# Half-size transfers in turn, five chunks ahead, and one chunk at a time on VectorE

## The chip, the core and the metric

The kernel runs on one core of one Trainium2 chip. The metric is the device time of one execution in microseconds (us), lower is better. A core has five engines that run their own instruction queues and meet at semaphores: TensorE (PE in the profile), VectorE (DVE), ScalarE (ACT), GpSimd (POOL) and SyncE (SP), which here only issues DMA transfers.

## What is computed

`x` has shape (2048, 64, 16, 16) in fp32: 2048 images of 64 channels and 16 x 16 pixels, 134 MB. Each image is normalised in groups of two neighbouring channels, goes through a hexagonal convolution (three 4 x 4 kernels with five taps each and a stride of 2, after a border that is filled by wrapping pixels around), is masked, and is added to the input:

```python
def _gn(v, G=32, eps=1e-5):           # groups of 2 channels x 256 pixels
    g = v.reshape(B_, G, C_ // G, H_, W_)
    m, s = mean(g), var(g)            # over (2, 3, 4)
    return ((g - m) / jnp.sqrt(s + eps)).reshape(v.shape)

xp = pad(x, 1); xp = xp.at[:, :, DST_R, DST_C].set(xp[:, :, SRC_R, SRC_C])
up    = conv(xp, w_up    * UP,    b_up)       # 4x4, stride 2, 5 taps used
left  = conv(xp, w_left  * LEFT,  b_left)
right = conv(xp, w_right * RIGHT, b_right)
out[:, :, 0::2, 0::2], out[:, :, 1::2, 0::2], out[:, :, 1::2, 1::2] = up, left, right
return x + out * OUT_MASK             # with x = _gn(x) as conv input
```

The input is read once and the output, of the same size, written once: 269 MB in all.

## The kernel before, in words

The images are cut into 64 chunks (`NCHUNK`) of 32 images. A chunk lies in SBUF as 128 partitions (two images x 64 channels) by 16 pairs (`G`) of 256 pixels, 2 MB. `xs` has 8 slots (`SLOTS`) for chunks; a chunk is loaded into its slot, its results are added to it in place, and the slot is stored. The stages of a chunk k are these.

- SP issues every transfer. `load` (L182) fetches one chunk in one transfer; `store` (L186) waits until GpSimd has added all four banks of the chunk (`bank_added`) and writes it. After store k, the load of chunk k + 7 waits for the store of chunk k - 1 (L211, the same slot). The first chunk comes in quarters. The bias vectors come in six tiny transfers on the same queue, behind chunk 2 (L202).
- VectorE takes the statistics: eight `bn_stats` (L233) for a chunk. `moments` (L237) makes the variance from them in six small operations on 128 x 16 (or 48) values, ScalarE takes the square root (`root`, L312), and `norms` (L258) makes the factor and the offset in five more. Each of them that needs the one before waits on a semaphore. The `bn_stats` of chunk k + 1 are written between these small operations of chunk k (`bn(ahead, ...)`), so `stats` has two buffers.
- `normalise` writes the normalised chunk into one of two buffers `tn`: pairs 0 to 7 on VectorE (L281), 8 to 15 on ScalarE (L320). It waits until the convolution of chunk k - 2 has read that buffer (`wait_t_free`, L158).
- GpSimd wraps the border with five copies (`wrap`, L414).
- TensorE (L462) runs 240 matmuls for a chunk into four PSUM banks; there are two sets of four, one for even, one for odd chunks. Banks 0 and 1 are full halfway, banks 2 and 3 at the end. A tiny matmul (L473) opens each chunk.
- ScalarE empties a bank with the bias into `res` (`evacuate`, L343, ten activations for a chunk). `res` holds one chunk, so it waits until GpSimd has added the same bank of the chunk before.
- GpSimd adds `res` to the slot in `xs` (`add`, L404, twelve strided tensor_tensor operations).

The order of the work is written out by hand. ScalarE: root k, evacuate k - 2, normalise k. GpSimd: add k - 2, wrap k. VectorE: moments k, norms k (both with the statistics of k + 1 in between), normalise k. The small operations of VectorE that this document counts are L241 (shuffle), L245, L246, L247, L249, L254 (variance), then after the root L262 (reciprocal), L265, L269, L272, L276 (offset).

Of the kernel before, what the change touches and what calls it, by code (L numbers as in the profile page):

```python
# [7 lines left out]
F32 = mybir.dt.float32  # L8
# [5 lines left out]
P = 128  # L14
B, C, HW = 2048, 64, 16
PIX = HW * HW
G = 16
NCHUNK = B // (2 * G)
SLOTS = 8
LAG = 2  # L20
# [41 lines left out]


QUARTER = G // 4


WRAPS = [
# [22 lines left out]
def hex_conv(nc, x, w_up, b_up, w_left, b_left, w_right, b_right, out):  # L90
    ctx = ExitStack()
    with ctx:
        def sb(name, shape, dt):
            return ctx.enter_context(nc.sbuf_tensor(name, shape, dt))

        def sem(name):
            return ctx.enter_context(nc.semaphore(name))
# [8 lines left out]
        ident = sb("ident", [P, C], F32)  # L106
        blank = sb("blank", [P, P], F16)
        bias = sb("bias", [P, 3], F32)
        stats = sb("stats", [P, 2, G, 3], F32)
        mate = sb("mate", [P, G, 3], F32)  # L110
        gap = sb("gap", [P, G], F32)
        gap2 = sb("gap2", [P, G], F32)
# [16 lines left out]
            at = 2 * C * 16 + C * (NT * W_AT[t][1] + n)  # L129
            return tn[1][W_AT[t][0]:W_AT[t][0] + C, at:at + C]  # L130

        loaded = [sem(f"loaded{s}") for s in range(SLOTS)]
        stored = [sem(f"stored{s}") for s in range(SLOTS)]
        w_loaded = [sem(f"w_loaded{t}") for t in range(3)]
        b_loaded = sem("b_loaded")
        quarter = [sem(f"quarter{n}") for n in range(3)]
        cleared = sem("cleared")
        identity = sem("identity")
        edges_clear = sem("edges_clear")
# [39 lines left out]

        @block.sync  # L180
        def _(sp):
            def load(k):  # L182
                s = k % SLOTS
                sp.dma_start(xs[:, s, :].rearrange("p (g q) -> p g q", g=G), x_dram[k]).then_inc(loaded[s], 16)

            def store(k):  # L186

                s = k % SLOTS
                sp.wait_ge(bank_added, NB * (k + 1))
                sp.dma_start(out_dram[k], xs[:, s, :].rearrange("p (g q) -> p g q", g=G)).then_inc(stored[s], 16)  # L190

            for t, w in enumerate((w_up, w_left, w_right)):
                sp.dma_start(w_raw(t), w.rearrange("o c a b -> o (c a b)")).then_inc(w_loaded[t], 16)
            for n in range(4):
                pairs = slice(QUARTER * n, QUARTER * (n + 1))
                sp.dma_start(xs[:, 0, :].rearrange("p (g q) -> p g q", g=G)[:, pairs],
                             x_dram[0][:, pairs]).then_inc(quarter[n] if n < 3 else loaded[0], 16)
            load(1)
            load(2)
            for t, b in enumerate((b_up, b_left, b_right)):  # L200
                for h in range(2):
                    sp.dma_start(bias[C * h:C * h + C, t:t + 1],  # L202
                                 b.rearrange("(o a) -> o a", a=1)).then_inc(b_loaded, 16)

            for k in range(3, SLOTS):
                load(k)

            for k in range(NCHUNK - 1):
                store(k)
                if 0 < k < NCHUNK - SLOTS + 1:  # L210
                    sp.wait_ge(stored[(k - 1) % SLOTS], 16 * ((k - 1) // SLOTS + 1))  # L211
                    load(k + SLOTS - 1)
            for half in range(2):
                pairs = slice(G // 2 * half, G // 2 * (half + 1))
                sp.wait_ge(bank_added, NB * NCHUNK + 2 * half)
                sp.dma_start(out_dram[NCHUNK - 1][:, pairs],
                             xs[:, SLOTS - 1, :].rearrange("p (g q) -> p g q", g=G)[:, pairs]
                             ).then_inc(stored[SLOTS - 1], 16)
            for s in range(SLOTS):
                sp.wait_ge(stored[s], 16 * (NCHUNK // SLOTS + (s == SLOTS - 1)))  # L220

        @block.vector
        def _(dve):
            def bn(k, u0, u1):

                if k >= NCHUNK:
                    return
                s = k % SLOTS
                if u0 == 0 and k:
                    dve.wait_ge(loaded[s], 16 * (k // SLOTS + 1))  # L230
                for u in range(u0, u1):
                    both = view(xs, (s * G + 2 * u) * PIX, [(1, PIX), (PIX, 2)])
                    last = nc.vector.bn_stats(stats[:, k % 2, 2 * u:2 * u + 2].rearrange("p g a -> p (g a)"), both)  # L233
                if u1 == G // 2:
                    last.then_inc(bn_done, 1)

            def moments(k, ahead):  # L237

                done = STAT_OPS * k
                own = stats[:, k % 2]  # L240
                nc.vector.stream_shuffle(mate[:].rearrange("p g a -> p (g a)"), own.rearrange("p g a -> p (g a)"),  # L241
                                         [p ^ 1 for p in range(32)]).then_inc(stat_step, 1)
                bn(ahead, 0, 1)
                dve.wait_ge(stat_step, done + 1)
                nc.vector.tensor_tensor(gap[:], own[:, :, 1], mate[:, :, 1], ALU.subtract).then_inc(stat_step, 1)  # L245
                nc.vector.tensor_tensor(m2[:], own[:, :, 2], mate[:, :, 2], ALU.add).then_inc(stat_step, 1)  # L246
                nc.vector.tensor_tensor(msum[:], own[:, :, 1], mate[:, :, 1], ALU.add).then_inc(stat_step, 1)  # L247
                dve.wait_ge(stat_step, done + 2)
                nc.vector.scalar_tensor_tensor(gap2[:], gap[:], float(PIX // 2), gap[:],  # L249
                                               op0=ALU.mult, op1=ALU.mult).then_inc(stat_step, 1)  # L250
                bn(ahead, 1, 2)
                dve.wait_ge(stat_step, done + 5)

                nc.vector.scalar_tensor_tensor(var[:], gap2[:], EPS * GROUP, m2[:],  # L254
                                               op0=ALU.add, op1=ALU.add).then_inc(var_ready, 1)
                bn(ahead, 2, 4)

            def norms(k, ahead):  # L258

                done = STAT_OPS * k + 5  # L260
                dve.wait_ge(std_ready, k + 1)
                nc.vector.reciprocal(small[:, 0], std[:]).then_inc(stat_step, 1)  # L262
                bn(ahead, 4, 5)
                dve.wait_ge(stat_step, done + 1)
                nc.vector.scalar_tensor_tensor(small[:, 1], var[:], -0.5 / GROUP, small[:, 0],  # L265
                                               op0=ALU.mult, op1=ALU.mult).then_inc(stat_step, 1)
                bn(ahead, 5, 6)
                dve.wait_ge(stat_step, done + 2)
                nc.vector.tensor_tensor(small[:, 2], small[:, 1], small[:, 0], ALU.mult).then_inc(stat_step, 1)  # L269
                bn(ahead, 6, 7)  # L270
                dve.wait_ge(stat_step, done + 3)
                nc.vector.scalar_tensor_tensor(rstd[:], small[:, 2], 1.5, small[:, 0],  # L272
                                               op0=ALU.add, op1=ALU.mult).then_inc(stat_step, 1)
                bn(ahead, 7, 8)
                dve.wait_ge(stat_step, done + 4)
                nc.vector.scalar_tensor_tensor(nmr[:], msum[:], -0.5, rstd[:],  # L276
                                               op0=ALU.mult, op1=ALU.mult).then_inc(norm_ready, 1)
# [10 lines left out]
                t_pairs(k % 2, k % SLOTS, 0, pairs).then_inc(t_dve, 1)  # L288

            for n in range(4):  # L290
                if n < 3:
                    dve.wait_ge(quarter[n], 16)
                else:
                    dve.wait_ge(loaded[0], 16)
                bn(0, QUARTER // 2 * n, QUARTER // 2 * (n + 1))
            dve.wait_ge(bn_done, 1)
            moments(0, NCHUNK)
            norms(0, NCHUNK)
            normalise(0, GD0)
            bn(1, 0, G // 2)  # L300
            dve.wait_ge(bn_done, 2)

            for k in range(1, NCHUNK):
                moments(k, k + 1)
                norms(k, k + 1)
                normalise(k)
                if k + 1 < NCHUNK:
                    dve.wait_ge(bn_done, k + 2)

        @block.scalar  # L310
        def _(act):
            def root(k):  # L312
                act.wait_ge(var_ready, k + 1)
                nc.scalar.activation(std[:], var[:], ACT.Sqrt, scale=1.0 / GROUP).then_inc(std_ready, 1)  # L314
# [15 lines left out]
            def evacuate(k, b, j):  # L330
# [15 lines left out]
                    at += cols  # L346
                last.then_inc(bank_empty, 1)

            act.wait_ge(identity, 1)
            nc.scalar.activation(warm[:], ident[0:C, 0:1], ACT.Sqrt)  # L350
            for t in range(3):
# [5 lines left out]
            root(0)  # L357
            normalise(0, GD0)

            root(1)  # L360
            normalise(1, GD)
            act.wait_ge(b_loaded, 16 * 6)
            for k in range(LAG, NCHUNK):
                root(k)
                for j in range(NB):
                    evacuate(k - LAG, k % 2, j)
                normalise(k, GD)
            for k in range(NCHUNK - LAG, NCHUNK):
                for j in range(NB):
                    evacuate(k, k % 2, j)  # L370

        @block.gpsimd
        def _(pool):
# [141 lines left out]
```

## Time and profile before

| | |
|---|---|
| median of 3 runs | 743.91 us (743.77 to 744.04) |
| profiled execution: time, span | 743.65 us, 741.8 us (granted TensorE clock 0.993) |
| busy PE / DVE / ACT / POOL | 656.3 / 667.6 / 574.5 / 487.5 us |
| DMA | 269.6 MB, mean 363 GB/s over the span |
| DMA busy share by 40ths | 9 tenths or more in all but the last slice (6) |

The profile is of one execution. Its time lies 1.85 us above its span (743.65 less 741.8) and 0.26 us below the median of the runs. Busy times are a union of an engine's instructions; an instruction that waits for something inside the engine still counts as busy, so a longer duration of the same operation at another place is a wait too. A timeline row gives start, duration, engine, line, operation, output and input, and in brackets how long the engine was idle before it and what ended that.

### The profile page before, as it was taken

To read this page: it belongs to the slowest core of one execution; us is meant where nothing else is said; L and a number is where in the kernel's file an instruction comes from. 1 tells how busy PE (TensorE), PEld (TensorE's weight loads), DVE (VectorE), ACT (ScalarE), POOL (GpSimd) and SP (SyncE) were. 2 spreads that over 40 slices of the span, in tenths; PEclk is the share of its full clock that TensorE was granted. 3 is DMA by queue.
4 is the path that set the end of the run, shared out by engine and by line. 5 is a ranking of instruction groups with operands and counts; after the bars stand their busy time and mean duration, and the time that the engine had idled before them with its cause. 6 is when DMAs were issued, how large, how long until landed. Compare 5 with 4: busy or idle time off the path is not lost.

```text
span 741.8 us, 35919 instructions
## 1 busy us (share of the span) xinstructions
PE 656.3 (88%) x15484; PEld 602.5 (81%) x15484; DVE 667.6 (90%) x1793; ACT 574.5 (77%) x1235; POOL 487.5 (66%) x1109
## 2 busy tenths in 40 slices
PE   1699999999998898898898988988988988989893
PEld 1589999999887887887887887878878878878883
DVE  4999999999889999999999999999999999999940
ACT  3398888888787787787787877877877877878782
POOL 1178777778567576676675675676766766766784
PEclk9999999999999999999999999999999999999998
DMA  9999999999999999999999999999999999999996
GB/s 275 339 349 380 379 376 372 373 360 364 362 374 378 369 372 373 369 377 371 374 363 376 380 368 374 369 374 369 375 377 364 378 365 378 370 373 374 369 327 229
DMA packets 265017, 269.60 MB, mean 363 GB/s; under 512 B 2640, under 2 KB 264784, under 8 KB 264976
## 3 DMA queue, kind: packets, MB, share of 16 engines
q1 hardware_dynamic: 264976, 269.23, 105.8%
q14 instruction: 37, 0.30, 0.1%
q8 instruction: 4, 0.07, 0.0%
HBM read 135.01 MB, written 134.22 MB: 363 GB/s over the span
## 4 chain that ended last, share of the span: by engine, by line
DMA 70%; DVE 18%; POOL 3%; PE 3%; ACT 2%; SPq 1%; issue 1%; POOLq 0%; ACTq 0%
DMA xs<-in_x 43%; DMA out<-xs 27%; DVE stats L233 9%; DVE tn L281 4%; POOL xs L404 3%; PE bank L462 3%; ACT res L343 1%; ACT tn L320 1%; DVE small L265 1%; DVE rstd L272 1%; SPq L190 1%; DVE nmr L276 0%; DVE small L269 0%; DVE m L246 0%; POOL tn L414 0%
## 5 line engine op out<-in xcount | busy, mean ns | idle before, releaser
L462 PE MATMUL bank<-tn,wts 64*64 64x192 f32 (+1 forms) x15360 | 647.0, 325 | 0.0
L462 PEld LDWEIGHTS bank<-tn,wts 64*64 64x64 f32 x15360 | 593.1, 137 | 34.5
L404 POOL TENSOR_TENSOR xs<-res,xs 128x192 f32<-128x192 f32 (+6 forms) x775 | 387.4, 539 | 71.5 <-ACT res L343 70.9
L233 DVE BATCH_NORM_STATS2 stats<-xs 128x6 f32<-128x512 f32 x512 | 347.2, 691 | 43.2 <-DMA xs<-in_x 43.2
L343 ACT ACTIVATE res<-bank,bias 64x512 f32<-64x512 f32 (+5 forms) x640 | 302.0, 472 | 17.3 <-PE bank L462 7.6
L320 ACT ACTIVATE tn<-xs,nmr,rstd 128x256 f32<-128x256 f32 x511 | 258.9, 591 | 9.2 <-DVE nmr L276 7.7
L414 POOL COPY tn<-tn 128x128 f32<-128x128 f32 (+2 forms) x320 | 97.6, 361 | 168.7 <-ACT tn L320 168.7
L281 DVE TENSOR_SCALAR tn<-xs,rstd,nmr 128x256 f32<-128x256 f32 x513 | 197.2, 454 | 2.3
L314 ACT ACTIVATE std<-var 128x16 f32<-128x16 f32 x64 | 13.8, 216 | 127.4 <-DVE var L254 127.4
L473 PEld LDWEIGHTS bank<-blank 128*128 128x128 f16 x64 | 6.1, 95 | 86.4 <-issue 82.6
L473 PE MATMUL bank<-blank 128*128 128x2 f16 x64 | 11.2, 175 | 67.6 <-POOL tn L414 67.6
L265 DVE SCALAR_TENSOR_TENSOR small<-var,small 128x16 f32<-128x16 f32 x64 | 30.4, 475 | 0.1
L272 DVE SCALAR_TENSOR_TENSOR rstd<-small 128x16 f32<-128x16 f32 x64 | 28.1, 438 | 0.1
L276 DVE SCALAR_TENSOR_TENSOR nmr<-msum,rstd 128x16 f32<-128x16 f32 x64 | 22.7, 355 | 0.1
L246 DVE TENSOR_TENSOR m<-stats,mate 128x16 f32<-128x16 f32 x64 | 21.8, 340 | 0.0
L247 DVE TENSOR_TENSOR msum<-stats,mate 128x16 f32<-128x16 f32 x64 | 21.1, 330 | 0.0
L249 DVE SCALAR_TENSOR_TENSOR gap<-gap 128x16 f32<-128x16 f32 x64 | 16.2, 254 | 0.0
L262 DVE RECIPROCAL small<-std 128x16 f32<-128x16 f32 x64 | 14.9, 233 | 0.7 <-ACT std L314 0.7
L245 DVE TENSOR_TENSOR gap<-stats,mate 128x16 f32<-128x16 f32 x64 | 14.1, 221 | 0.1
L269 DVE TENSOR_TENSOR small<-small 128x16 f32<-128x16 f32 x64 | 14.0, 219 | 0.1
L241 DVE STREAM_SHUFFLE mate<-stats 128x48 f32<-128x48 f32 x64 | 12.8, 201 | 0.0
L254 DVE SCALAR_TENSOR_TENSOR var<-gap,m 128x16 f32<-128x16 f32 x64 | 11.2, 175 | 0.1
(18 smaller groups left out, 17.0 us busy)
## 6 DMA issues: line engine op xcount, KB each, us to landing
xs<-in_x SPq DMA_DIRECT2D x63, 2048.0 KB, 16.8
out<-xs SPq DMA_DIRECT2D x63, 2048.0 KB, 17.0
xs<-in_x SPq DMA_DIRECT2D x4, 512.0 KB, 7.8
out<-xs SPq DMA_DIRECT2D x2, 1024.0 KB, 5.2
tn<-in_L_conv_w_up SPq DMA_DIRECT2D x1, 256.0 KB, 3.6
tn<-in_L_conv_w_left SPq DMA_DIRECT2D x1, 256.0 KB, 4.0
tn<-in_L_conv_w_right SPq DMA_DIRECT2D x1, 256.0 KB, 5.2
bias<-in_L_conv_b_up SPq DMA_DIRECT2D x2, 0.2 KB, 8.6
```

Source lines behind the costliest of these rows:

```text
L233: last = nc.vector.bn_stats(stats[:, k % 2, 2 * u:2 * u + 2].rearrange("p g a -> p (g a)"), both)
L246: nc.vector.tensor_tensor(m2[:], own[:, :, 2], mate[:, :, 2], ALU.add).then_inc(stat_step, 1)
L247: nc.vector.tensor_tensor(msum[:], own[:, :, 1], mate[:, :, 1], ALU.add).then_inc(stat_step, 1)
L265: nc.vector.scalar_tensor_tensor(small[:, 1], var[:], -0.5 / GROUP, small[:, 0], op0=ALU.mult, op1=ALU.mult).then_inc(stat_step, 1)
L272: nc.vector.scalar_tensor_tensor(rstd[:], small[:, 2], 1.5, small[:, 0], op0=ALU.add, op1=ALU.mult).then_inc(stat_step, 1)
L276: nc.vector.scalar_tensor_tensor(nmr[:], msum[:], -0.5, rstd[:], op0=ALU.mult, op1=ALU.mult).then_inc(norm_ready, 1)
L281: last = nc.vector.tensor_scalar(t_image(b, g), x_image(s, g), rstd[:, g:g + 1], nmr[:, g:g + 1], ALU.mult, ALU.add)
L320: last = nc.scalar.activation(t_image(k % 2, g), x_image(k % SLOTS, g), ACT.Identity, bias=nmr[:, g:g + 1], scale=rstd[:, g:g + 1])
L343: last = nc.scalar.activation(res[onto, BANK_AT[j] + at:BANK_AT[j] + at + cols], psum[NB * b + j][banks, at:at + cols], ACT.Identity, bias ...
L404: last = nc.gpsimd.tensor_tensor(onto, frm, onto, ALU.add)
L414: last = nc.gpsimd.tensor_copy(view(tn[b], dst, [(T_PAIR, G)] + [(d, n) for d, _, n in dims]), view(tn[b], src, [(T_PAIR, G)] + [(d, n) fo ...
L462: last = nc.tensor.matmul(psum[bank + j][to:to + C, at:at + cols], wts[first:first + C, NT * rect[0] + n, :], taps(b, rect, tap, first), s ...
```

## The change

SP now moves every chunk in two halves of eight pairs (1 MB each) with a semaphore for each half of a slot. Chunks 0 to 4 are asked for at the start (`AHEAD` = 5). After that SP issues for each chunk k: store of the first half of k, load of the first half of k + 5, store of the second half, load of the second half. Both halves of a store wait for the whole chunk, except for the last chunk. A load of chunk n waits for the store of chunk n - 8, which is k - 3. The bias vectors move to ScalarE's DMA queue, ahead of its first instruction.

VectorE no longer takes the statistics of the next chunk between the small operations. For each chunk it waits for a half, takes four `bn_stats`, waits for the other, takes four, then does moments, norms and normalise, and only then goes to the next chunk.

ScalarE's order becomes root k, normalise k, evacuate k - 1. GpSimd's and TensorE's code is unchanged.

```diff
+HALF = (slice(0, G // 2), slice(G // 2, G))
+AHEAD = 5
 ...
-        stats = sb("stats", [P, 2, G, 3], F32)
+        stats = sb("stats", [P, G, 3], F32)
 ...
+            for k in range(1, AHEAD):
+                for half in range(2):
+                    load(k, half)
+
+            for k in range(NCHUNK):
+                n = k + AHEAD
+                for half in range(2):
+                    sp.wait_ge(bank_added, NB * (k + 1) if k < NCHUNK - 1 else NB * k + 4 + 2 * half)
+                    store(k, half)
+                    if n < NCHUNK:
+                        if n >= SLOTS:
+                            sp.wait_ge(stored[n % SLOTS], 32 * (n // SLOTS))
+                        load(n, half)
 ...
-            def moments(k, ahead):
+            def moments(k):
                 done = STAT_OPS * k
-                own = stats[:, k % 2]
+                own = stats
+                dve.wait_ge(bn_done, k + 1)
                 nc.vector.stream_shuffle(mate...)
-                bn(ahead, 0, 1)
 ...
             for k in range(1, NCHUNK):
-                moments(k, k + 1)
-                norms(k, k + 1)
+                for half in range(2):
+                    dve.wait_ge(loaded[half][k % SLOTS], 16 * (k // SLOTS + 1))
+                    bn(k, G // 4 * half, G // 4 * (half + 1))
+                moments(k)
+                norms(k)
                 normalise(k)
 ...
-            root(1)
-            normalise(1, GD)
             act.wait_ge(b_loaded, 16 * 6)
-            for k in range(LAG, NCHUNK):
+            for k in range(1, NCHUNK):
                 root(k)
+                normalise(k, GD)
                 for j in range(NB):
-                    evacuate(k - LAG, k % 2, j)
-                normalise(k, GD)
-            for k in range(NCHUNK - LAG, NCHUNK):
-                for j in range(NB):
-                    evacuate(k, k % 2, j)
+                    evacuate(k - 1, (k - 1) % 2, j)
+            for j in range(NB):
+                evacuate(NCHUNK - 1, (NCHUNK - 1) % 2, j)
```

## Rows read from the trace of the kernel before

**Rows 1.** Windows: length, busy time by engine, granted clock, DMA share, GB/s.
```profile
15.00:20.00 5.00, 0.00 (x0) 0.00 (x0) 4.47 (x20) 2.98 (x7) 0.00 (x0) 1.00 1.10 349
...
200.00:690.00 490.00, 439.93 (x10412) 403.58 (x10412) 459.42 (x1217) 384.89 (x822) 328.35 (x738) 1.00 1.07 372
```

**Rows 2.** Waits from 200 to 700 us: total, times, longest.
```profile
DVE stats L233 <- DMA xs<-in_x: 31.1, 45, 1.3
```

**Rows 3.** Timeline of the first chunk, with nothing else between: start, duration, instruction.
```profile
14.94 0.20 DVE L241 STREAM_SHUFFLE mate<-stats 128x48 f32<-128x48 f32 x1
15.18 0.18 DVE L245 TENSOR_TENSOR gap<-stats,mate 128x16 f32<-128x16 f32 x1
...
15.65 0.17 DVE L254 SCALAR_TENSOR_TENSOR var<-gap,m 128x16 f32<-128x16 f32 x1
15.86 0.22 ACT L314 ACTIVATE std<-var 128x16 f32<-128x16 f32 x1 [5.68 <-DVE var L254]
16.11 0.25 DVE L262 RECIPROCAL small<-std 128x16 f32<-128x16 f32 x1 [0.28 <-ACT std L314]
16.40 0.18 DVE L265 SCALAR_TENSOR_TENSOR small<-var,small 128x16 f32<-128x16 f32 x1
...
17.24 3.00 DVE L281 TENSOR_SCALAR tn<-xs,rstd,nmr 128x256 f32<-128x256 f32 x9
20.15 4.92 DVE L233 BATCH_NORM_STATS2 stats<-xs 128x6 f32<-128x512 f32 x8
...
22.69 12.22 PE L462 MATMUL bank<-tn,wts 64*64 64x288 f32 x240
...
25.11 0.20 DVE L241 STREAM_SHUFFLE mate<-stats 128x48 f32<-128x48 f32 x1
25.80 0.70 DVE L233 BATCH_NORM_STATS2 stats<-xs 128x6 f32<-128x512 f32 x1 [0.48 <-DMA xs<-in_x]
```

**Rows 4.** Timeline of a period in the middle: normalise, wrap, VectorE beside it.
```profile
342.50 3.08 DVE L281 TENSOR_SCALAR tn<-xs,rstd,nmr 128x256 f32<-128x256 f32 x8
...
346.75 1.49 POOL L414 COPY tn<-tn 128x128 f32<-128x128 f32 x5 [2.29 <-ACT tn L320]
...
347.12 0.42 DVE L246 TENSOR_TENSOR m<-stats,mate 128x16 f32<-128x16 f32 x1
347.46 0.42 DVE L247 TENSOR_TENSOR msum<-stats,mate 128x16 f32<-128x16 f32 x1
```

**Rows 5.** Timeline of GpSimd alone, the third copy of that wrap.
```profile
347.45 0.41 POOL L414 COPY tn<-tn 128x128 f32<-128x128 f32 x1
```

**Rows 6.** Timeline of the same period: convolution, emptying, a small operation.
```profile
348.49 10.05 PE L462 MATMUL bank<-tn,wts 64*64 64x288 f32 x240
...
348.94 4.87 ACT L343 ACTIVATE res<-bank,bias 128x480 f32<-128x480 f32 x10
...
350.65 0.47 DVE L265 SCALAR_TENSOR_TENSOR small<-var,small 128x16 f32<-128x16 f32 x1
```

**Rows 7.** Timeline of GpSimd: adds 1 to 3, 4 to 8, 10 to 12 of that chunk.
```profile
349.66 2.04 POOL L404 TENSOR_TENSOR xs<-res,xs 128x288 f32<-128x288 f32 x3 [1.41 <-ACT res L343]
...
351.64 2.51 POOL L404 TENSOR_TENSOR xs<-res,xs 128x192 f32<-128x192 f32 x5
...
354.55 1.19 POOL L404 TENSOR_TENSOR xs<-res,xs 128x64 f32<-128x64 f32 x3
```

**Rows 8.** Timeline at the last chunk, whose small operations stand alone on VectorE.
```profile
707.96 1.51 POOL L414 COPY tn<-tn 128x128 f32<-128x128 f32 x5 [2.33 <-ACT tn L320]
...
708.26 0.18 DVE L265 SCALAR_TENSOR_TENSOR small<-var,small 128x16 f32<-128x16 f32 x1
708.47 0.27 DVE L269 TENSOR_TENSOR small<-small 128x16 f32<-128x16 f32 x1
...
709.35 4.98 DVE L281 TENSOR_SCALAR tn<-xs,rstd,nmr 128x256 f32<-128x256 f32 x8
```

**Rows 9.** Timeline of GpSimd in the same stretch, the first eight adds.
```profile
709.42 4.76 POOL L404 TENSOR_TENSOR xs<-res,xs 128x288 f32<-128x288 f32 x8
```

**Rows 10.** Timeline: two bias transfers on SP, and the last convolution.
```profile
20.28 1.24 SPq L202 DMA_DIRECT2D bias<-in_L_conv_b_left  x2
...
719.79 10.07 PE L462 MATMUL bank<-tn,wts 64*64 64x288 f32 x240
```

More of the change, by code:

```diff
@@ L130, in w_used @@
             return tn[1][W_AT[t][0]:W_AT[t][0] + C, at:at + C]
-        loaded = [sem(f"loaded{s}") for s in range(SLOTS)]
+        loaded = [[sem(f"loaded{s}_{half}") for s in range(SLOTS)] for half in range(2)]
         stored = [sem(f"stored{s}") for s in range(SLOTS)]
@@ L135, in hex_conv @@
         b_loaded = sem("b_loaded")
-        quarter = [sem(f"quarter{n}") for n in range(3)]
+        quarter = [sem(f"quarter{n}") for n in range(2)]
         cleared = sem("cleared")
@@ L181, in _, with part, load, store @@
         def _(sp):
[L182 to L190, printed above, removed]
+            def part(dram, k, pairs):
+                return dram[k][:, pairs], xs[:, k % SLOTS, :].rearrange("p (g q) -> p g q", g=G)[:, pairs]
+            def load(k, half):
+                frm, to = part(x_dram, k, HALF[half])
+                sp.dma_start(to, frm).then_inc(loaded[half][k % SLOTS], 16)
+            def store(k, half):
+                to, frm = part(out_dram, k, HALF[half])
+                sp.dma_start(to, frm).then_inc(stored[k % SLOTS], 16)
             for t, w in enumerate((w_up, w_left, w_right)):
@@ L194, in _ @@
             for n in range(4):
[L195 to L218, printed above, removed]
+                frm, to = part(x_dram, 0, slice(QUARTER * n, QUARTER * (n + 1)))
+                sp.dma_start(to, frm).then_inc((quarter[n // 2], loaded[n // 2][0])[n % 2], 16)
+            for k in range(1, AHEAD):
[10 more added lines that the diff above has]
+                        load(n, half)
             for s in range(SLOTS):
-                sp.wait_ge(stored[s], 16 * (NCHUNK // SLOTS + (s == SLOTS - 1)))
+                sp.wait_ge(stored[s], 32 * (NCHUNK // SLOTS))
         @block.vector
@@ L224, in bn @@
             def bn(k, u0, u1):
-                if k >= NCHUNK:
-                    return
                 s = k % SLOTS
-                if u0 == 0 and k:
-                    dve.wait_ge(loaded[s], 16 * (k // SLOTS + 1))
                 for u in range(u0, u1):
                     both = view(xs, (s * G + 2 * u) * PIX, [(1, PIX), (PIX, 2)])
-                    last = nc.vector.bn_stats(stats[:, k % 2, 2 * u:2 * u + 2].rearrange("p g a -> p (g a)"), both)
+                    last = nc.vector.bn_stats(stats[:, 2 * u:2 * u + 2].rearrange("p g a -> p (g a)"), both)
                 if u1 == G // 2:
                     last.then_inc(bn_done, 1)
-            def moments(k, ahead):
+            def moments(k):
                 done = STAT_OPS * k
-                own = stats[:, k % 2]
-                nc.vector.stream_shuffle(mate[:].rearrange("p g a -> p (g a)"), own.rearrange("p g a -> p (g a)"),
+                own = stats
+                dve.wait_ge(bn_done, k + 1)
+                nc.vector.stream_shuffle(mate[:].rearrange("p g a -> p (g a)"), own[:].rearrange("p g a -> p (g a)"),
                                          [p ^ 1 for p in range(32)]).then_inc(stat_step, 1)
-                bn(ahead, 0, 1)
                 dve.wait_ge(stat_step, done + 1)
@@ L250, in moments @@
                                                op0=ALU.mult, op1=ALU.mult).then_inc(stat_step, 1)
-                bn(ahead, 1, 2)
                 dve.wait_ge(stat_step, done + 5)
@@ L255, in moments, with norms @@
                                                op0=ALU.add, op1=ALU.add).then_inc(var_ready, 1)
-                bn(ahead, 2, 4)
-            def norms(k, ahead):
+            def norms(k):
                 done = STAT_OPS * k + 5
@@ L262, in norms @@
                 nc.vector.reciprocal(small[:, 0], std[:]).then_inc(stat_step, 1)
-                bn(ahead, 4, 5)
                 dve.wait_ge(stat_step, done + 1)
@@ L266, in norms @@
                                                op0=ALU.mult, op1=ALU.mult).then_inc(stat_step, 1)
-                bn(ahead, 5, 6)
                 dve.wait_ge(stat_step, done + 2)
                 nc.vector.tensor_tensor(small[:, 2], small[:, 1], small[:, 0], ALU.mult).then_inc(stat_step, 1)
-                bn(ahead, 6, 7)
                 dve.wait_ge(stat_step, done + 3)
@@ L273, in norms @@
                                                op0=ALU.add, op1=ALU.mult).then_inc(stat_step, 1)
-                bn(ahead, 7, 8)
                 dve.wait_ge(stat_step, done + 4)
@@ L290, in _ @@
             for n in range(4):
[L291 to L294, printed above, removed]
+                dve.wait_ge((quarter[n // 2], loaded[n // 2][0])[n % 2], 16)
                 bn(0, QUARTER // 2 * n, QUARTER // 2 * (n + 1))
-            dve.wait_ge(bn_done, 1)
-            moments(0, NCHUNK)
-            norms(0, NCHUNK)
+            moments(0)
+            norms(0)
             normalise(0, GD0)
-            bn(1, 0, G // 2)
-            dve.wait_ge(bn_done, 2)
             for k in range(1, NCHUNK):
-                moments(k, k + 1)
-                norms(k, k + 1)
+                for half in range(2):
[3 more added lines that the diff above has]
+                norms(k)
                 normalise(k)
-                if k + 1 < NCHUNK:
-                    dve.wait_ge(bn_done, k + 2)
         @block.scalar
@@ L347, in evacuate @@
                 last.then_inc(bank_empty, 1)
+            for t, b in enumerate((b_up, b_left, b_right)):
+                for h in range(2):
+                    act.dma_start(bias[C * h:C * h + C, t:t + 1],
+                                 b.rearrange("(o a) -> o a", a=1)).then_inc(b_loaded, 16)
             act.wait_ge(identity, 1)
```

## The prediction

> **What bounds the kernel now.** I read the time windows first. From 200 to 690 us the DMA engines are busy throughout and move 372 GB/s; when only loads ran, at 15 to 20 us, it was 349 [rows 1]. A chunk is 2.097 MB in and as much out, so 4.194 MB / 372 GB/s = 11.27 us is what a chunk costs in transfers. The view of waits says the same from the other side: VectorE's first `bn_stats` of a chunk waits for its load once per chunk, 31.1 us in 45 chunks, 0.69 us each [rows 2]. VectorE could therefore go round in 11.27 - 0.69, about 10.6 us at most. TensorE needs 10.05 us for a chunk [rows 6]. So DMA is the bound, and three engines stand less than 1.3 us behind it. Any change to VectorE's loop must be asked whether it still fits into 11.27 us.
>
> **VectorE's new loop, without company.** I count from N, the start of a chunk's normalise on VectorE, to the same point a chunk later. The first chunk of the kernel before shows each piece with nothing between. Nine tensor_scalars from 17.24 to 20.15 are 0.323 us each, so eight take 2.59. Eight `bn_stats` from 20.15 to the shuffle at 25.11: 4.96. Shuffle to L245, 14.94 to 15.18: 0.24. L245 to normalise, 15.18 to 17.24: 2.06, the trip to ScalarE's root included [all rows 3]. Sum 9.85 us. On this count the loop fits, and DMA stays the bound. It is the count I don't believe, for the following reason.
>
> **VectorE beside GpSimd.** L246 and L247 take 0.42 us each in the middle of the run, start 0.34 us apart, and run beside wrap copies of 0.41 us, the third of which starts at 347.45 when L247 starts at 347.46 [rows 4, 5]. In the first chunk, with GpSimd idle, four of them and a wait fit between 15.18 and 15.65, about 0.12 us each [rows 3]. So VectorE's small operations with two inputs take turns with GpSimd's: one for one. Beside adds it is the same: L265 takes 0.47 instead of 0.18 [rows 6, 3], and the last chunk's eight tensor_scalars take 4.98 us beside eight adds of 4.76, against 2.59 alone [rows 8, 9, 3]. `bn_stats` is not touched: the eight from 20.15 on keep their pace though a wrap ran in the middle of them. What the interleaving bought was this: the small operations were spread, one between two `bn_stats` of 0.62 us, so that GpSimd's turn passed behind a `bn_stats`. The change puts nine two-input operations in a row.
>
> The Trainium skill (SBUF — State Buffer, "Who interferes with whom") says that a VectorE instruction with two SBUF inputs, or in a two-port mode, and a GpSimd instruction that reads SBUF shut each other out for the whole instruction, and that one with a single input outside those modes doesn't. The trace agrees, by the 0.42 against 0.17 to 0.18 us above.
>
> **Where GpSimd will be.** Its code is the same, but add k - 1 no longer waits for ScalarE to pass the next root: the banks are emptied straight after normalise. N to the start of wrap is 342.50 to 346.75, 4.25 us; the wrap takes 1.49 [rows 4]; the adds then follow at N + 5.75, since by then ScalarE has emptied bank 0 (about 0.7 us after its normalise ends). The first three adds take until 351.64, 1.98 us; adds 4 to 8 2.5; the last three end 6.08 us after the first began [rows 7]. So adds run from N + 5.75 to N + 11.83. VectorE reaches L245 at N + 2.59 + 4.96 + 0.24 = N + 7.79, just after add 4 began (N + 7.73). Then, turn by turn:
> - L245, L246, L247, L249, L254 end with adds 4 to 8, at N + 10.2 (351.64 + 2.51 is 4.49 after the first add; less the 0.05 by which neighbours overlap). Alone they took 0.64.
> - The root and back: from L254's end at 15.82 to L262's start at 16.11, 0.29, and L262 to L265 0.29 more [rows 3]: N + 10.8.
> - L265, L269, L272 end with adds 10, 11, 12: the last at N + 11.83. L276 is free again: 0.2, and normalise starts at **N + 12.05**.
>
> The neighbours: ScalarE's ten activations take 4.87 [rows 6], from N + 4.1 to N + 9.0, ahead of the root at N + 10.2: covered by 1.2 us. TensorE starts a chunk 1.74 us after the wrap began (346.75 to 348.49 [rows 4, 6]) and ends 10.05 later, N + 16.0; bank 2 is wanted at N + 12.05 + 4.1 + 2.1 = N + 18.3, so it may be 2.2 us slower and cost nothing. The waits for a free `tn` buffer and for `res` are long past by then. Period 12.05 against 11.27: VectorE with GpSimd becomes the bound.
>
> The value hangs on which add VectorE meets first. One turn earlier gives 11.85, one turn later about 12.25; these are the bounds.
>
> **The transfers.** At 12.05 us a chunk DMA idles 0.8 us of it. A load is issued when chunk k is added, N(k+1) + 11.8, and lands with its store at most 11.3 later; it is wanted at N(k+4) + 2.6, that is N(k+1) + 38.7. Five ahead are enough. What halves do to the rate no row shows. The lower bound I take is all at the one-directional 349 GB/s: 12.02 us a chunk, still under 12.05. A gain in rate would be worth nothing. At the start, chunk 2 has landed by 25.80 [rows 3]; two more at 349 GB/s, 6.0 us each, end at 37.8, then DMA idles until the first store near 39.5. That costs nothing either, as chunk 5 is wanted only past 66. The six bias issues take 0.62 us each on a queue [rows 10], 3.7 us on ScalarE at the start; ScalarE stood idle 5.68 us ahead of the first root [rows 3], which covers it. Without that cover it would be up to 3.7 once.
>
> **The sum.** N(0) = 17.24. N(1) = 20.15 + 4.96 + 0.24 + 2.06 = 27.41, no adds yet. The first convolution ends at 34.91 [rows 3] and holds ScalarE back a little, I add 0.2. Then 62 periods: 27.41 + 0.2 + 62 x 12.05 = 774.7. From the last normalise to the end: 4.25 + 1.74 + 10.07, and from the end of the convolution (719.79 + 10.07 = 729.86 [rows 10]) to the end of the span, 741.84, 11.98: 28.04. Span 802.7; with the 1.85 between span and time 804.6. Against the profiled execution's 743.65 that is +61; its time lies 0.26 under the median of the runs, which doesn't matter here. Forecast **804 us**, with periods of 11.85 to 12.25: 792 to 817.
>
> **The rivals.**
> - *GpSimd gives way (faster).* If it is the adds that wait for the VectorE operations and not the reverse, the loop takes 9.85 us, DMA bounds again, and the change gains at the end: the first store at 39.5, then 59 loads and 59 stores of 5.635 us end at 704; four `bn_stats` (2.5) and 2.3 more put N(63) at 709; +28.0 +1.85 = 739 us. This decides as soon as VectorE's loop stays below 11.27 us, so if turns cost it under 1.4 us instead of 2.2. For it speaks L265 at 708.26, which slipped in ahead of a copy and took 0.18 [rows 8]; against it L269 behind it with 0.27, and the 4.98 us of the tensor_scalars. The same page of the Trainium skill says that the one that issues first holds the pair. 6%.
> - *Half of the turns slip.* As at 708.26, dependent operations get in ahead at times. With three or four turns spared the period is about 11.4: 27.6 + 62 x 11.4 + 28.0 + 1.85 = 764 us. 12%.
> - *DMA loses with halves, or the turns cost more.* Alternating 1 MB transfers drop the rate below 348 GB/s, or adds stretched by VectorE's operations lengthen the row of turns (eight took 4.76 here against 4.49 in the middle, [rows 9, 7]): period 12.5, 832 us. 9%.
> - *TensorE slows.* It idles 2 us of each period; at half its clock for part of it, a convolution could pass 12.2 us. From 12.3 on it sets the period; 13 us would give 863. 3%.
> - *The change does nothing that counts*: DMA-bound with the old ends, 742 to 744: 2%.
>
> The forecast itself has 68%. Low and high reach to periods of 11.55 and 12.4: 775 and 827; this leaves out about 20%. About 0.2% is what runs of this kernel can tell from no change. Faster 0.06, same 0.02, slower 0.92.
>
> **What the changed profile would show.** The share of DMA falls to 0.93 or so of its earlier value and GB/s to about 348. VectorE's wait for loads goes to nearly nothing, and the chain of work runs through VectorE's small operations and GpSimd's adds. L245 to L254 have durations of 0.35 to 0.65 us, L276 about 0.2. The distance between two normalise groups on VectorE is 12.05. ScalarE's root waits for the variance, never for its own emptying. If `bn_stats` still waits for loads every chunk, the forecast is wrong.

## The result and the profile after

The changed kernel takes 794.3 us (793.38 to 795.26, 4 runs) against 743.97 for the kernel before in the same runs: ratio 1.067, 95% interval 1.066 to 1.069. The profiled execution took 793.74 us with a span of 791.9. The forecast was 804, slower, with a range of 775 to 827.

The page of the changed kernel: span, GB/s in 40 slices, and the shares of the chain of work that ended last.

```profile
span 791.9 us, 36045 instructions
...
GB/s 264 309 316 361 349 351 361 348 354 357 351 346 366 354 347 362 357 348 359 357 348 356 351 351 359 356 350 353 351 348 363 353 355 354 357 345 359 269 212 212
...
DVE 91%; issue 2%; ACT 2%; PE 1%; DMA 1%; POOL 1%; SPq 0%; POOLq 0%; ACTq 0%
```

Of the kernel before, the chain was this:

```profile
DMA 70%; DVE 18%; POOL 3%; PE 3%; ACT 2%; SPq 1%; issue 1%; POOLq 0%; ACTq 0%
```

It ran over DMA for 70% of the span; now VectorE has 91% of it. The transfers fell from 372 GB/s in the middle [rows 1] to 354, because less was asked of them (4.194 MB in each loop of 11.86 us):

```profile
200.00:690.00 490.00, 437.84 (x9922) 397.56 (x9926) 466.36 (x1158) 367.50 (x787) 299.62 (x706) 0.95 1.06 354
```

The view of waits has no line any more for VectorE's `bn_stats` waiting for a load in the middle of the run (31.1 us before [rows 2]). One round of the loop, VectorE, ScalarE and GpSimd's adds (the lines are numbered anew: L235 to L243 are the old L245 to L254, L250 to L260 the old L262 to L276, L265 the old L281, L223 the `bn_stats`, L384 the adds):

```profile
401.70 5.76 POOL L384 TENSOR_TENSOR xs<-res,xs 128x288 f32<-128x288 f32 x12
...
403.89 0.40 DVE L235 TENSOR_TENSOR gap<-stats,mate 128x16 f32<-128x16 f32 x1
404.21 0.54 DVE L236 TENSOR_TENSOR m<-stats,mate 128x16 f32<-128x16 f32 x1
404.67 0.66 DVE L237 TENSOR_TENSOR msum<-stats,mate 128x16 f32<-128x16 f32 x1
405.25 0.43 DVE L239 SCALAR_TENSOR_TENSOR gap<-gap 128x16 f32<-128x16 f32 x1
405.71 0.40 DVE L243 SCALAR_TENSOR_TENSOR var<-gap,m 128x16 f32<-128x16 f32 x1
406.14 0.22 ACT L293 ACTIVATE std<-var 128x16 f32<-128x16 f32 x1 [1.29 <-DVE var L243]
406.39 0.25 DVE L250 RECIPROCAL small<-std 128x16 f32<-128x16 f32 x1 [0.28 <-ACT std L293]
406.68 0.50 DVE L252 SCALAR_TENSOR_TENSOR small<-var,small 128x16 f32<-128x16 f32 x1
407.21 0.28 DVE L255 TENSOR_TENSOR small<-small 128x16 f32<-128x16 f32 x1
...
407.52 0.17 DVE L257 SCALAR_TENSOR_TENSOR rstd<-small 128x16 f32<-128x16 f32 x1
407.73 0.18 DVE L260 SCALAR_TENSOR_TENSOR nmr<-msum,rstd 128x16 f32<-128x16 f32 x1
...
407.95 2.68 DVE L265 TENSOR_SCALAR tn<-xs,rstd,nmr 128x256 f32<-128x256 f32 x8
```

The adds run from 401.70 to 407.46. Every two-input operation that falls in that time is long (0.40 to 0.66, and 0.50 and 0.28), and the two behind its end take 0.17 and 0.18, as in the first chunk of the kernel before [rows 3]. GpSimd's adds one by one, numbers 4, 8, 11 and 12 of the twelve:

```profile
403.63 0.62 POOL L384 TENSOR_TENSOR xs<-res,xs 128x192 f32<-128x192 f32 x1
...
405.61 0.47 POOL L384 TENSOR_TENSOR xs<-res,xs 128x128 f32<-128x128 f32 x1
...
406.74 0.41 POOL L384 TENSOR_TENSOR xs<-res,xs 128x96 f32<-128x96 f32 x1
407.11 0.35 POOL L384 TENSOR_TENSOR xs<-res,xs 128x64 f32<-128x64 f32 x1
```

Each of VectorE's long operations ends 0.03 to 0.04 us after one of them: L235 at 404.29 after add 4 (404.25), L243 at 406.11 after add 8 (406.08), L252 at 407.18 after add 11 (407.15), L255 at 407.49 after add 12 (407.46); L236, L237 and L239 go with adds 5, 6 and 7 in the same way. ScalarE waited 1.29 us for the variance, so it wasn't late. N(k) is the start of VectorE's normalise of chunk k, as in the prediction. N(1) is 28.30 and N(63) is 763.90 in this trace, so the loop is (763.90 - 28.30) / 62 = 11.86 us.

### The profile page after: what moved, and what is told of

Same layout as the page of the kernel before. It is cut to its first block, busy times and chain, and to the rows that moved or that the text cites. A ratio compares the mean times of both kernels' runs of the same rounds, so it can differ in the third digit from the quotient of the medians.

```text
span 791.9 us, 36045 instructions
## 1 busy us (share of the span) xinstructions
PE 684.1 (86%) x15484; PEld 621.4 (78%) x15484; DVE 719.4 (91%) x1793; ACT 574.1 (72%) x1235; POOL 466.1 (59%) x1109
## 4 chain that ended last, share of the span: by engine, by line
DVE 91%; issue 2%; ACT 2%; PE 1%; DMA 1%; POOL 1%; SPq 0%; POOLq 0%; ACTq 0%
DVE stats L223 39%; DVE tn L265 21%; DVE msum L237 4%; DVE small L252 4%; DVE m L236 4%; DVE var L243 3%; DVE gap L235 3%; DVE gap L239 3%; DVE small L255 2%; DVE small L250 2%; ACT std L293 2%; DVE mate L232 2%; DVE rstd L257 2%; DVE nmr L260 2%; PE bank L442 1%
## 5 line engine op out<-in xcount | busy, mean ns | idle before, releaser
L442 PE MATMUL bank<-tn,wts 64*64 64x192 f32 (+1 forms) x15360 | 674.0, 333 | 0.0
L442 PEld LDWEIGHTS bank<-tn,wts 64*64 64x64 f32 x15360 | 612.0, 141 | 42.6
L384 POOL TENSOR_TENSOR xs<-res,xs 128x192 f32<-128x192 f32 (+6 forms) x775 | 369.2, 521 | 3.6 <-ACT res L322 3.5
L223 DVE BATCH_NORM_STATS2 stats<-xs 128x6 f32<-128x512 f32 x512 | 318.0, 697 | 10.5 <-DMA xs<-in_x 10.5
L265 DVE TENSOR_SCALAR tn<-xs,rstd,nmr 128x256 f32<-128x256 f32 x513 | 171.8, 410 | 2.6 <-DVE nmr L260 0.3
L237 DVE TENSOR_TENSOR msum<-stats,mate 128x16 f32<-128x16 f32 x64 | 40.6, 634 | 0.0
L236 DVE TENSOR_TENSOR m<-stats,mate 128x16 f32<-128x16 f32 x64 | 33.9, 530 | 0.0
L250 DVE RECIPROCAL small<-std 128x16 f32<-128x16 f32 x64 | 16.2, 253 | 18.1 <-ACT std L293 18.1
L252 DVE SCALAR_TENSOR_TENSOR small<-var,small 128x16 f32<-128x16 f32 x64 | 28.7, 448 | 2.2
L243 DVE SCALAR_TENSOR_TENSOR var<-gap,m 128x16 f32<-128x16 f32 x64 | 25.2, 394 | 2.2
L239 DVE SCALAR_TENSOR_TENSOR gap<-gap 128x16 f32<-128x16 f32 x64 | 26.8, 419 | 0.0
L235 DVE TENSOR_TENSOR gap<-stats,mate 128x16 f32<-128x16 f32 x64 | 24.7, 386 | 2.2
L255 DVE TENSOR_TENSOR small<-small 128x16 f32<-128x16 f32 x64 | 17.5, 273 | 2.2
L257 DVE SCALAR_TENSOR_TENSOR rstd<-small 128x16 f32<-128x16 f32 x64 | 11.9, 186 | 2.2
L260 DVE SCALAR_TENSOR_TENSOR nmr<-msum,rstd 128x16 f32<-128x16 f32 x64 | 11.3, 177 | 2.2
## 6 DMA issues: line engine op xcount, KB each, us to landing
xs<-in_x SPq DMA_DIRECT2D x126, 1024.0 KB, 10.8
```

The costliest lines, as they stand in the source:

```text
L223: last = nc.vector.bn_stats(stats[:, 2 * u:2 * u + 2].rearrange("p g a -> p (g a)"), both)
L265: last = nc.vector.tensor_scalar(t_image(b, g), x_image(s, g), rstd[:, g:g + 1], nmr[:, g:g + 1], ALU.mult, ALU.add)
L384: last = nc.gpsimd.tensor_tensor(onto, frm, onto, ALU.add)
L442: last = nc.tensor.matmul(psum[bank + j][to:to + C, at:at + cols], wts[first:first + C, NT * rect[0] + n, :], taps(b, rect, tap, first), s ...
```

## The experiments

All times are medians; the ratio is to the kernel before in the same runs.

| run | time, us | ratio (95%) |
|---|---|---|
| the change | 794.3 | 1.067 (1.066 to 1.069) |
| no_adds (doesn't compute the result) | 740.6 | 0.996 (0.994 to 0.997) |
| interleave | 816.9 | 1.102 (1.096 to 1.109) |
| gd7 | 800.5 | 1.076 (1.074 to 1.078) |
| gd9 | 781.0 | 1.050 (1.048 to 1.051) |
| gd10 | 785.5 | 1.056 (1.055 to 1.058) |
| no_newton (leaves out a step of accuracy) | 748.7 | 1.006 (1.004 to 1.007) |
| scalar_undone | 824.4 | 1.107 (1.106 to 1.109) |
| vector_alone | 823.2 | 1.106 (1.104 to 1.108) |
| transfers_alone | 761.5 | 1.024 (1.022 to 1.025) |
| transfers_7 | 741.3 | 0.996 (0.995 to 0.998) |
| change_7 | 795.2 | 1.069 (1.067 to 1.070) |
| short_row | 743.3 | 1.000 (0.998 to 1.001) |

The theory to be tested ("turns"): each two-input operation of VectorE that meets GpSimd's adds waits for one of them to end, and a row of nine such operations makes VectorE's loop longer than DMA's 11.27 us. The rivals: the row is slow by itself; VectorE is simply full; the transfers; ScalarE's new order. The edits shift the line numbers of some runs by a few; the names of the tiles tell which operation a row shows.

**Without the adds.**

```diff
             def add(k, j, g0=0, pairs=G):
+                nc.gpsimd.memset(sink[:, at0:at0 + 1], 0.0).then_inc(bank_added, 1)
+                return
```

> The changed kernel without GpSimd's additions: each bank's twelve-part add is replaced by a write of one value to a scratch column that signals the same semaphore, so the output is the input alone (the convolution is computed and not added). Turn theory: the nine two-input operations take 0.17 to 0.18 us each, the loop would be 9.9 us, so DMA bounds at 11.27: 735 to 742 us. Rival (the row of dependent operations and the trip to ScalarE's root is what costs, GpSimd is not in it): the period stays 11.9 and the time 790 to 795.

Measured: 740.6 us. VectorE in the middle of that run:

```profile
403.44 2.53 DVE L224 BATCH_NORM_STATS2 stats<-xs 128x6 f32<-128x512 f32 x4 [1.26 <-DMA xs<-in_x]
...
406.26 0.18 DVE L236 TENSOR_TENSOR gap<-stats,mate 128x16 f32<-128x16 f32 x1
...
408.31 2.67 DVE L266 TENSOR_SCALAR tn<-xs,rstd,nmr 128x256 f32<-128x256 f32 x8
```

From the first small operation to normalise it takes 2.05 us (406.26 to 408.31), where the changed kernel takes 4.06 (403.89 to 407.95). So 2.0 us of each loop belong to GpSimd's adds, and without them VectorE waits for loads again (1.26 us). The row by itself is not slow.

**VectorE gets less or more to do.** `GD` is the number of pairs that VectorE normalises; ScalarE has the rest of the sixteen.

```diff
-GD = 8
+GD = 7      # gd7;  9 in gd9, 10 in gd10
```

> The changed kernel with VectorE normalising seven pairs of a chunk and ScalarE nine. Turn theory: VectorE comes to its small operations 0.3 us earlier and the adds start 0.5 us later, so it meets the third to the seventh and then the ninth to the twelfth: period 12.0, 802 us, though VectorE has less work. Rival (VectorE is simply full): 0.32 x 62 = 20 us less, 774 us.

> The changed kernel with VectorE normalising ten pairs of a chunk and ScalarE six, instead of eight and eight. Turn theory: ScalarE ends about 1 us earlier, so wrap and adds start about 1 us earlier against VectorE, which itself comes to its small operations 0.65 us later; it meets the last six adds only (from the seventh on), and its last four small operations are free: period 11.5, 768 us. Rival (VectorE is simply full, work added to it is time added): 0.65 x 62 = 40 us more, 834 us.

> The changed kernel with nine pairs on VectorE and seven on ScalarE. Turn theory: wrap at N + 3.7, adds at N + 5.2, the first small operation at N + 8.2 in the sixth add, five turns to the tenth, then one in the twelfth, three free: loop 11.65 us, 780 us. Rival (VectorE is simply full): 794 + 20 = 814 us.

Measured: 800.5, 785.5 and 781.0 us. "VectorE is simply full" gave 774, 834 and 814; it has the wrong sign three times. With one pair less the kernel is 6 us slower, with one pair more 13 us faster. The forecasts of the turns (802 for seven pairs, 768 for ten, 780 for nine) hold for seven and nine. In gd7 the adds start later and still run when the last small operation comes, which isn't free any more:

```profile
405.13 5.72 POOL L384 TENSOR_TENSOR xs<-res,xs 128x288 f32<-128x288 f32 x12
...
410.60 0.28 DVE L260 SCALAR_TENSOR_TENSOR nmr<-msum,rstd 128x16 f32<-128x16 f32 x1
```

In gd9 the period is 413.35 - 401.69 = 11.66 us:

```profile
401.69 3.00 DVE L265 TENSOR_SCALAR tn<-xs,rstd,nmr 128x256 f32<-128x256 f32 x9
...
405.38 1.50 POOL L394 COPY tn<-tn 128x128 f32<-128x128 f32 x5 [4.45 <-ACT tn L299]
406.84 5.75 POOL L384 TENSOR_TENSOR xs<-res,xs 128x288 f32<-128x288 f32 x12
...
409.84 0.62 DVE L235 TENSOR_TENSOR gap<-stats,mate 128x16 f32<-128x16 f32 x1
...
412.51 0.18 DVE L252 SCALAR_TENSOR_TENSOR small<-var,small 128x16 f32<-128x16 f32 x1
...
413.35 1.06 DVE L265 TENSOR_SCALAR tn<-xs,rstd,nmr 128x256 f32<-128x256 f32 x3
```

The wrap and the adds come earlier, since ScalarE has seven pairs, and after the root all four small operations are free (0.18). For ten pairs the forecast was 17 us too low. The trace shows a thing that it had wrong: the wrap waits for both halves of the normalised chunk, and now VectorE's half ends last.

```profile
404.38 3.32 DVE L265 TENSOR_SCALAR tn<-xs,rstd,nmr 128x256 f32<-128x256 f32 x10
...
407.77 1.50 POOL L394 COPY tn<-tn 128x128 f32<-128x128 f32 x5 [4.52 <-DVE tn L265]
```

I had counted ScalarE's six pairs alone, 3.07 us; the wrap starts at N + 3.39 instead. These 0.3 us in 62 chunks have the size of the miss, but no run tells them from the rest of that forecast, whose period of 11.5 was not worked out turn by turn.

**Three of the nine taken out.**

```diff
-                nc.vector.reciprocal(small[:, 0], std[:]).then_inc(stat_step, 1)
-                ... small[:, 1], small[:, 2] and rstd from it
+                nc.vector.reciprocal(rstd[:], std[:]).then_inc(stat_step, 1)
```

> The changed kernel without the refinement of 1/sqrt: three two-input operations of norms are taken out and the reciprocal goes straight to rstd. It computes the same but a step of accuracy. Turn theory: VectorE's loop becomes 11.87 - 0.8 = 11.1 us, just under DMA's 11.27, so DMA bounds and the time is 738 to 744 us. Rival (ScalarE's ring or GpSimd sets the 11.9): 790 us or more.

Measured: 748.7 us. The first and the last normalise of the loop on VectorE:

```profile
27.18 2.67 DVE L257 TENSOR_SCALAR tn<-xs,rstd,nmr 128x256 f32<-128x256 f32 x8
...
720.47 2.67 DVE L257 TENSOR_SCALAR tn<-xs,rstd,nmr 128x256 f32<-128x256 f32 x8
```

(720.47 - 27.18) / 62 = 11.18 us, 0.1 above what was worked out and 0.68 less than in the changed kernel. The rival's 790 is out. The total is above the 738 to 744, because I let DMA set it. VectorE's loop still sets the end, with its start of 27.2 and its tail of 28.0, and has 88% of the chain in the page of this run, DMA 1%.

The kernel before doesn't go round in 11.27 us from the start: its normalise of chunk 1 begins at 31.64 and that of chunk 16 at 183.60, 10.13 us a chunk, on loads that lie ready. A loop of 11.18 us can't catch up in that way.

**ScalarE's order undone, and VectorE's part alone.**

The edit of scalar_undone:

```diff
-            for k in range(1, NCHUNK):
+            for k in range(LAG, NCHUNK):
                 root(k)
+                for j in range(NB):
+                    evacuate(k - LAG, k % 2, j)
                 normalise(k, GD)
 ...
-                    evacuate(k - 1, (k - 1) % 2, j)
```

vector_alone is the kernel before with `moments(k)` and `norms(k)` of the change, so with no `bn_stats` between the small operations.

> The changed kernel with ScalarE's order alone undone: root k, evacuate k - 2, normalise k. Turn theory, from the root: adds begin 0.85 us after it, so two small operations and all eight tensor_scalars take turns with adds (normalise ends 6.35 after the root instead of 3.6), then bn_stats 4.96, and the variance is free: period 12.2, 817 us with the later wrap at the end. Rival (ScalarE's new order is what slows the change): below 794, down to 745.

> The kernel before with VectorE's part of the change alone: one chunk at a time, whole transfers, ScalarE's old order. Turn theory: as with ScalarE's order undone, 12.2 us a chunk, 815 to 820 us; the transfers make no difference. Rival (transfers matter): more than 5 us from that run.

Measured: 824.4 us, 7 above the forecast, and 823.2, 3 above the upper end of its range, and within 2 us of each other though one has half transfers five ahead and the other whole ones. ScalarE's new order is therefore worth 30 us to the change (824.4 to 794.3), by where it puts the adds:

```profile
400.53 4.95 DVE L223 BATCH_NORM_STATS2 stats<-xs 128x6 f32<-128x512 f32 x8
...
405.76 0.18 DVE L235 TENSOR_TENSOR gap<-stats,mate 128x16 f32<-128x16 f32 x1
...
407.30 6.25 POOL L387 TENSOR_TENSOR xs<-res,xs 128x288 f32<-128x288 f32 x12 [2.45 <-ACT res L322]
407.41 0.76 DVE L257 SCALAR_TENSOR_TENSOR rstd<-small 128x16 f32<-128x16 f32 x1
408.20 0.53 DVE L260 SCALAR_TENSOR_TENSOR nmr<-msum,rstd 128x16 f32<-128x16 f32 x1
408.77 4.17 DVE L265 TENSOR_SCALAR tn<-xs,rstd,nmr 128x256 f32<-128x256 f32 x8
...
412.87 0.70 DVE L223 BATCH_NORM_STATS2 stats<-xs 128x6 f32<-128x512 f32 x1
```

Here the variance is free (0.18), but two small operations and the eight tensor_scalars (4.17 us instead of 2.68) take turns: 412.87 - 400.53 = 12.34 us a chunk.

**VectorE's part undone.**

```diff
-            def moments(k):
+            def moments(k, ahead):
 ...
+                bn(ahead, 0, 1)
                 dve.wait_ge(stat_step, done + 1)
```

> The changed kernel with VectorE's part alone undone: the statistics of the next chunk stand between the small operations again, with two stats buffers. Halves, five ahead, ScalarE's order and the bias queue stay. Turn theory: the turns pass behind bn_stats, the loop of VectorE falls to about 10.3 us and DMA bounds at 11.27 us a chunk; some 738 us, 0.993 of the kernel before. Rival (halves or five ahead starve the transfers): 760 to 795, VectorE waiting for loads and DMA idle in the middle.

Measured: 816.9 us where 738 was expected, the largest miss of all runs: worse than the change, and neither by turns nor, for the most part, by the transfers; in its middle VectorE waits for no load. What goes round is ScalarE's work and the root's way through VectorE:

```profile
409.97 4.05 ACT L312 ACTIVATE tn<-xs,nmr,rstd 128x256 f32<-128x256 f32 x8 [3.08 <-DVE nmr L270]
...
413.93 4.86 ACT L335 ACTIVATE res<-bank,bias 128x480 f32<-128x480 f32 x10
...
418.81 0.22 ACT L306 ACTIVATE std<-var 128x16 f32<-128x16 f32 x1
...
422.14 4.05 ACT L312 ACTIVATE tn<-xs,nmr,rstd 128x256 f32<-128x256 f32 x8 [3.11 <-DVE nmr L270]
```

In the new order ScalarE empties banks ahead of the root, and normalise hangs on the root by way of VectorE's five operations. Normalise 3.96, emptying 4.88, then root to normalise 3.33: 12.17 us, a ring with no slack in it. The 3.33 are long because four `bn_stats` stand among the five operations; in the changed kernel the same way takes 1.81 (406.14 to 407.95). The small operations themselves are short again, though the adds run from 403.46 to 409.20:

```profile
403.46 5.74 POOL L397 TENSOR_TENSOR xs<-res,xs 128x288 f32<-128x288 f32 x12
...
408.39 0.16 DVE L263 TENSOR_TENSOR small<-small 128x16 f32<-128x16 f32 x1
```

So the turns did pass behind `bn_stats`, as expected, and the time was lost elsewhere. Emptying ahead of the root, with the statistics between, is the worse pairing; the two parts of the change belong together. That ring is what the next run tells from the transfers.

**The transfers alone** (the run above, with ScalarE's old order as well).

> The kernel before with the transfers of the change alone: halves in turn, five ahead, bias on ScalarE's queue; VectorE's statistics between the small operations and ScalarE's order (root, evacuate k - 2, normalise) as before. Ring theory: without ScalarE's new order nothing but DMA is near 11.27 us; the time is DMA's, 738 to 743 us. Rival (it was the transfers that made the run with the statistics interleaved slow, not ScalarE's order): 800 us or more.

Measured: 761.5 us. ScalarE's order accounts for 55 us of the run above (816.9 to 761.5), as the ring theory says, but this is 17 us above the kernel before, which it doesn't say. Of this run a window at the start, a wait in the middle, and the GB/s of the page:

```profile
36.00:46.00 10.00, 8.99 (x171) 8.15 (x175) 9.96 (x29) 8.80 (x20) 7.28 (x18) 0.83 0.35 114
```
```profile
DVE stats L227 <- DMA xs<-in_x: 85.6, 43, 2.3
```
```profile
GB/s 264 331 234 383 384 384 376 369 367 371 367 360 368 374 365 367 371 370 366 372 371 366 368 370 371 371 369 368 368 368 365 376 367 366 370 369 369 348 226 221
```

DMA is at 0.35 of its time for 10 us: the five chunks are in, and the first store is issued at 42.76. So I tried the depth by itself:

```diff
-AHEAD = 5
+AHEAD = 7
```

> The run with the transfers alone, but seven chunks ahead instead of five. Depth theory: with ScalarE emptying chunk k - 2 a chunk lives longer, and five ahead leaves DMA idle before the first store and loads late by 2 us in each chunk; with seven the time is that of the kernel before, 740 to 746 us. Rival (it is the halves that cost): it stays near 761.

> The changed kernel with seven chunks ahead instead of five. Turn theory: VectorE waits for no load in the middle, so the depth is worth nothing: 794 us, within 2. Rival (the depth or late loads hold the change back): below 788.

Measured: 741.3 with the transfers alone, 795.2 in the change. The five ahead cost 20 us in the one and nothing that can be measured in the other, since the change stores earlier and its VectorE waits for no load. With seven ahead the halves are even a little faster than the kernel before, 0.996 (0.995 to 0.998), though in the middle they move no more: 368 GB/s against 372 [rows 1]. The gain is at the ends. The page of this run:

```profile
GB/s 265 348 362 384 385 372 378 379 366 377 370 353 372 364 372 371 365 373 366 371 372 368 369 368 363 376 366 369 375 366 368 364 364 376 366 368 372 377 355 284
```

The last two slices are 355 and 284 GB/s; they were 327 and 229 in the kernel before. VectorE still waits for loads, 84.9 us in all between 200 and 700 us, as much as with five ahead (85.6), so that wait is not what the depth costs. The 20 us between the two runs lie at both ends: 234 against 362 GB/s in the third slice, 226 and 221 against 355 and 284 in the last two.

**All that helps the changed kernel at once.**

```diff
-GD = 8
+GD = 9
 ...
-AHEAD = 5
+AHEAD = 6
 ...      # and without the three operations, as in no_newton
```

> The changed kernel without the three refining operations, with nine pairs on VectorE and seven on ScalarE, and six chunks ahead. Turn theory: adds start 0.5 us earlier against the chunk, the small operations 0.3 us later, one or two turns fewer: loop 11.0 us, 28.3 + 62 x 11.0 + 28 + 1.9 = 740 us, just ahead of the kernel before, if DMA keeps 372 GB/s. Rival (more work for VectorE is more time): 748.7 + 20 = 769 us.

Measured: 743.3 us, level with the kernel before (0.998 to 1.001), 3 us above the forecast and far from the rival's 769. First and last normalise:

```profile
26.52 3.00 DVE L257 TENSOR_SCALAR tn<-xs,rstd,nmr 128x256 f32<-128x256 f32 x9
...
714.25 3.00 DVE L257 TENSOR_SCALAR tn<-xs,rstd,nmr 128x256 f32<-128x256 f32 x9
```

The loop is 687.73 / 62 = 11.09 us where 11.0 was expected, which is 62 x 0.09 = 5.6 us; the start and the tail gave part of it back (N(1) at 26.52, where 28.3 was put in the sum). Of all runs that compute the whole result only transfers_7 beats both kernels, by 0.4%.

## Why the prediction was right

**The bound.** Right in sign, mechanism and size. DMA was the bound, VectorE's loop grew past 11.27 us through turns with GpSimd, and DMA, depth and rate dropped out. no_adds shows the mechanism by taking away the other side, gd7 and gd9 by moving the phase against the direction of the load. One reading of the rows was too wide: three engines were said to stand less than 1.3 us behind DMA, and the rows show two, VectorE (0.69) and TensorE (10.05 of 11.27).

**The loop, 12.05 forecast, 11.86 measured.** This term was mis-sized by 0.19 us: 62 rounds were to take 747.1 us and took 735.6, which is 11.5 less. N(1) came 0.7 later than the 27.6 of the sum, and so the span fell 10.8 short of 802.7. In the round shown above, N is 396.03:

```profile
396.03 0.41 DVE L265 TENSOR_SCALAR tn<-xs,rstd,nmr 128x256 f32<-128x256 f32 x1
```

VectorE met the adds as forecast: its first two-input operation at N + 7.86 (forecast 7.79), in add 4, and the five of the variance in adds 4 to 8. What was wrong is the end of the adds, N + 11.43 instead of N + 11.83. They began 0.08 earlier than forecast, and they take 5.76 us where I gave them 6.08, from rows in which the first tensor_scalars of the chunk overlap them. Then L252 (the old L265) began in add 10 and ended only with add 11, L255 (the old L269) ended with add 12, and L257 (the old L272), which I had in add 12, was free. The earlier end gave 0.40, two free operations behind the adds instead of one took 0.27 back. That leaves 0.13 in this round of 11.92 us, and 0.19 in the mean of all 62. The prediction's lower bound of 11.85 was for another case, in which VectorE meets the adds one turn earlier; that the measured value lies beside it is chance.

**The five turns of the variance** were forecast at 2.4 us from L245 to the end of L254 (N + 7.79 to N + 10.2); L235 to L243 take 2.22 (403.89 to 406.11).

**The neighbours.** ScalarE idles 1.29 us ahead of the root, forecast 1.2. The tail is 791.9 - 763.90 = 28.0, forecast 28.04.

**Five ahead are enough**: right for the change (change_7: the same time), but only there; transfers_alone shows 20 us for it when the chunk lives longer. I did not see that condition.

**The bias at nothing**: the root was covered, but by less than was said. The six issues hold ScalarE from 0.73 to 6.62, 5.9 us and not 3.7; ScalarE's wait for the first variance shrank from 5.68 to 3.42.

```profile
3.53 3.09 ACTq L330 DMA_DIRECT2D bias<-in_L_conv_b_right  x2
```

N(0) came at 18.06 instead of 17.24: the first `bn_stats` waited for its data until 9.81 us, 9.08 before. Whether the bias issues on the other queue have a part in it stays open. With the same start as the change, N(0) is 17.49 in change_7, 17.51 in gd7 and 18.20 in gd10, so most of the 0.8 us is what it scatters from one execution to the next.

**TensorE's clock**: the 3% rival saw the fall of the clock, but not its size. The slowed convolutions took 11.33 us, below its 12.3, and cost nothing.

**GpSimd gives way**: it didn't; the twelve adds took 5.76 us here, 5.75 in gd9, 5.72 in gd7 and 5.74 in interleave, whichever small operations they met. Beside the tensor_scalars of scalar_undone they took 6.25, so there both sides pay. **Half of the turns slip**: of the eight turns that were forecast one fell away (L257), the other seven were whole.

**The range** was stated as 775 to 827 for periods of 11.55 and 12.4; by its own sum these give 774 and 826. It was said to leave out about 20%, but the five rivals, all priced outside it, add up to 32%. Neither bears on the outcome.

## What to carry to other kernels

When operations of two engines take turns, as VectorE's two-input operations and GpSimd's adds do here, each short dependent operation costs up to an instruction of the other engine (0.26 to 0.66 us in the rounds shown, instead of 0.17). Count how many fall into the other's busy stretch, and move the phase, that is, where in the loop the one meets the other, before the load (VectorE with one pair more was 13 us faster). An order written out by hand on two engines is one object: undoing the part that lost time here made the kernel slower by 23 us, for a ring of root, normalise and emptying closed on ScalarE. A loop only just shorter than the old bound still sets the end, with the start and the tail that it brings (no_newton: 11.18 us a chunk and 748.7 us in all).

## What the runs showed of the hardware

The granted clock of TensorE fell to the lower of its levels (1.2 GHz of 2.4) again and again in the changed kernel, 0.95 of the upper one on average in the middle against 1.00 before. Then a convolution takes 11.33 us instead of 10.07:

```profile
757.95 11.33 PE L442 MATMUL bank<-tn,wts 64*64 64x288 f32 x240
...
769.86 10.07 PE L442 MATMUL bank<-tn,wts 64*64 64x288 f32 x240
```

Ahead of the first of these TensorE had been idle for 1.69 us; with gaps of 1.50 us in gd9 (period 11.66) and 1.57 in gd10 (11.73) the clock stayed at its upper level all through the middle (1.00). gd7, interleave and scalar_undone, with periods from 11.97 to 12.34, all had 0.94, vector_alone 0.95. No run varies the gap alone, so what brings the clock down is not shown. It cost nothing here, since the gap of 1.69 us is longer than the 1.26 us that it adds to a convolution; in a kernel with a shorter gap it would count.
